# Layer 0 attention's last head and its row norm: squares and the weight row taken in column groups

## The reference, cut to what matters

```python
def rmsnorm(x, w, eps=1e-5):
    return (x * rsqrt(mean(x * x, axis=-1) + eps)) * w

x = layernorm(x)                                  # 625 x 768
qkv = rmsnorm(x, norm1_w) -> 12 heads of 64 columns
attn = softmax(qkv @ qkv.T / 8);  attn_out = attn @ qkv
out = x + attn_out                                # called z in the kernel
xf = rmsnorm(out, norm3_w)                        # called xf in the kernel
logits = xf @ gate_w.T ...                        # router, shared expert, 8 experts, top 2
```

## Time and profile before

| what | value |
|---|---|
| median of 3 runs | 1630.15 us (1621.01 to 1632.26) |
| the profiled execution | 1624.75 us |
| its span | 1623.2 us |
| TensorE busy | 1474.0 us, 91% |
| VectorE busy | 1275.0 us, 79% |
| ScalarE busy | 873.8 us, 54% |
| GpSimd busy | 331.8 us, 20% |
| granted TensorE clock, mean | 0.961 |

### The profile page before, as it was taken

The page is one execution under the profiler, slowest core; times in us unless marked ns, Lnnn a source line. Parts: engine busy times, 40 slices in busy tenths (PEclk is TensorE's granted clock), DMA queues, the critical chain, the costliest instruction groups (busy, mean ns, idle before and its releaser), DMA issues.

```text
span 1623.2 us, 36989 instructions
## 1 busy us (share of the span) xinstructions
PE 1474.0 (91%) x14673; PEld 1270.6 (78%) x14673; DVE 1275.0 (79%) x2196; ACT 873.8 (54%) x1235; POOL 331.8 (20%) x254
## 2 busy tenths in 40 slices
PE   7988868886999999999999889965999999999996
PEld 5666646664667899999999654445999999999995
DVE  8997767775565588888888779867988888888785
ACT  1113247775544567777665235554656666666651
POOL 0000405664030000000004037754600000000040
PEclk9999889998899999999999889978999999999999
DMA  7640000002375679888986011125888888888883
GB/s 201 159 120 1 1 10 1 1 1 79 120 223 174 229 277 289 305 308 292 296 301 225 26 32 33 33 88 195 294 304 290 297 286 301 297 293 291 296 264 102
DMA packets 55556, 297.61 MB, mean 183 GB/s; under 512 B 14063, under 2 KB 14319, under 8 KB 32433
## 3 DMA queue, kind: packets, MB, share of 16 engines
q1 hardware_dynamic: 41761, 263.23, 47.6%
q0 software_dynamic: 13712, 33.26, 7.5%
HBM read 264.07 MB, written 32.34 MB: 183 GB/s over the span
## 4 chain that ended last, share of the span: by engine, by line
PE 59%; DVE 7%; POOL 3%; ACT 2%; issue 2%; DMA 2%; SPq 0%; DVEq 0%; ACTq 0%
PE ps L744 14%; PE ps L723 9%; PE ps L725 9%; PE ps L727 9%; PE ps L2243 5%; PE ps L2226 5%; POOL wl L997 2%; PE ps L2355 2%; DMA ext<-in_units 2%; PE ps L756 1%; DVE wl L600 1%; PE ps L707 1%; DVE big L1875 1%; PE ps L2327 1%; PE ps L2297 1%
## 5 line engine op out<-in xcount | busy, mean ns | idle before, releaser
L723 PE MATMUL ps<-big,wh 128*128 128x176 f16 x2160 | 495.4, 239 | 10.6 <-DVE wl L600 8.5
L727 PE MATMUL ps<-big,wl 128*128 128x176 f16 x2160 | 495.4, 238 | 0.0
L725 PE MATMUL ps<-big,wh 128*128 128x176 f16 x2160 | 495.4, 238 | 0.0
L744 PE MATMUL ps<-big,wh 128*128 128x176 f16 x2160 | 262.8, 238 | 3.3 <-DVE big L634 3.3
L744 PE MATMUL ps<-big,wl 128*128 128x176 f16 x1080 | 248.9, 239 | 0.0
L600 DVE SCALAR_TENSOR_TENSOR wl<-ext,wh 128x2304 f16<-128x2304 f32 x90 | 229.6, 2552 | 1.7 <-issue 1.5
L600 DVE SCALAR_TENSOR_TENSOR wl<-raw,wh 128x2304 f16<-128x2304 f32 x90 | 229.5, 2550 | 0.0
L519 ACT ACTIVATE wh<-raw 128x2304 f16<-128x2304 f32 x90 | 190.6, 2119 | 59.2 <-PE ps L744 53.6
L723 PEld LDWEIGHTS ps<-big,wh 128*128 128x128 f16 x2160 | 208.3, 96 | 15.1 <-DVE wl L600 8.9
L519 ACT ACTIVATE wh<-ext 128x2304 f16<-128x2304 f32 x90 | 190.6, 2118 | 50.5 <-PE ps L744 33.1
L725 PEld LDWEIGHTS ps<-big,wh 128*128 128x128 f16 x2160 | 210.8, 98 | 0.2
(11 more groups left out here) (363 smaller groups left out, 2839.1 us busy)
## 6 DMA issues: line engine op xcount, KB each, us to landing
raw<-in_units SPq DMA_DIRECT2D x54, 1152.0 KB
ext<-in_units SPq DMA_DIRECT2D x54, 1152.0 KB
raw<-in_units SPq DMA_DIRECT2D x36, 1153.0 KB, 6.7
ext<-in_units SPq DMA_DIRECT2D x36, 1153.0 KB, 7.1
raw<-in_units_s SPq DMA_DIRECT2D x16, 769.0 KB, 4.5
ext<-in_units_s SPq DMA_DIRECT2D x16, 769.0 KB, 4.4
x_slots<-raw SPq DMA_DIRECT2D x1, 8976.0 KB
big<-x_slots POOLq DMA_DIRECT2D x17, 528.0 KB, 8.6
```

What stands on the lines that cost most here:

```text
L723: nc.tensor.matmul(o, wh[:, u % RING, w_], x_, start=c == 0 and m == 0, stop=False, skip_group_check=True)
L725: nc.tensor.matmul(o, wh[:, u % RING, w_], xTl[:, c, 0:ph.n], start=False, stop=False, skip_group_check=True)
L727: ins = nc.tensor.matmul(o, wl[:, u % RING, w_], x_, start=False, stop=c == KC - 1, skip_group_check=True)
L744: ins = nc.tensor.matmul(o, l_[:, u % RING, w_], r_, start=first and k == 0 and c % 2 == 0, stop=last and k == 2, skip_group_check=True)
```

## The change

Columns are cut at 256, 512, 704 and 768 (`PARTS`), that is behind heads 3, 7, 10 and 11.

- ScalarE squares columns 0 to 255 during head 6 and columns 256 to 511 during head 10, one tile in each step, behind that step's `weight_high`. It squares columns 512 to 703 behind the last `weight_high`, once head 10 has been added, and columns 704 to 767 behind the fence. The sums go to `st`, one number for each tile and group, and VectorE adds the four of them (a new reduction ahead of `mean_squares`).
- `sum_out(10)` is moved ahead of the last `weight_high` on ScalarE.
- VectorE computes `xf = z * vec` for columns 0 to 703 as soon as head 10 has been added. For head 11 the steps `fin` and `head_joined` are replaced by five VectorE instructions that multiply from PSUM and add into `z`. Then it computes the last 64 columns of `xf`. All of this stands ahead of the fence.
- `squares_asked` is gone. The scratch place of the fifth tile's squares moves to column 6700 of `big`.

```diff
+PARTS = (0, 4 * HD, 8 * HD, 11 * HD, D)
...
             weight_low(H * NT - 1)
             head_joined(H - 2)
-            head_joined(H - 1)
             fence(pool, F_MHA)
...
-            def squares():
-
-                count["sq"] += 1
-                act.wait_ge(s_var, count["sq"])
-                for t in range(NT):
-                    ins = nc.scalar.activation(junk[t], z[:, t, :], ACT.Square, accum_out=rs[:, 0, t:t + 1])
-                ins.then_inc(s_sq, 1)
+            def squares(g, t):
+
+                own = slice(PARTS[g], PARTS[g + 1])
+                nc.scalar.activation(junk[t][:, own], z[:, t, own], ACT.Square,
+                                     accum_out=st[:, t, g, 0:1]).then_inc(s_part, 1)
...
                 if t == 0 and h >= 2:
                     sum_out(h - 2)
+                if h in (6, 10):
+                    if t == 0:
+                        act.wait_ge(s_madd, h - 2)
+                    squares((h - 6) // 4, t)
+            sum_out(H - 2)
             weight_high(H * NT - 1)
-            sum_out(H - 2)
+            act.wait_ge(s_madd, H - 1)
+            for t in range(NT):
+                squares(2, t)
             sum_out(H - 1)
             fence(act, F_MHA)
...
-            squares()
+            act.wait_ge(s_madd, H)
+            for t in range(NT):
+                squares(3, t)
             root()
...
-                count["sq"] += 1
-                dve.wait_ge(s_sq, count["sq"])
+                dve.wait_ge(s_part, 4 * NT)
+                step(nc.vector.tensor_reduce(rs[:, 0, :], st[:, :, :, 0], AX.X, ALU.add))
                 nc.vector.tensor_scalar(rs[:, 0, :], rs[:, 0, :], 1.0 / D, eps, ALU.mult, ALU.add)\
...
             fin(H - 2)
-            fin(H - 1)
+
+            def row_weighted(n0, n1):
+
+                for t in range(NT):
+                    ins = nc.vector.tensor_tensor(xf[:, t, n0:n1], z[:, t, n0:n1], vec[:, 0, n0:n1], ALU.mult)
+                return ins
+
+            dve.wait_ge(s_vec[0], 32)
+            dve.wait_ge(s_madd, H - 1)
+            row_weighted(0, PARTS[3])
+            dve.wait_ge(s_mback, H)
+            for t in range(NT):
+                ins = nc.vector.scalar_tensor_tensor(
+                    out=z[:, t, PARTS[3]:D], in0=bank(7)[0:P, 128 + t * HD:128 + (t + 1) * HD],
+                    scalar=cols[:, 4 + (H - 1) % 2, t:t + 1], in1=z[:, t, PARTS[3]:D], op0=ALU.mult, op1=ALU.add)
+            ins.then_inc(s_madd, 1)
+            dve.wait_ge(s_madd, H)
+            step(row_weighted(PARTS[3], D))
             fence(dve, F_MHA)
...
-            squares_asked()
-            dve.wait_ge(s_vec[0], 32)
-            for t in range(NT):
-                ins = nc.vector.tensor_tensor(xf[:, t, :], z[:, t, :], vec[:, 0, :], ALU.mult)
-            step(ins)
             mean_squares(1e-5)
```

More of the change, by code:

```diff
@@ L159, in bass_gnn_moe_stack @@
         xsl = region(big, KC * T // 2, KC * T // 2).bitcast(F16).rearrange("p (c n) -> p c n", c=KC)
-        junk = [big[0:P, (t if t < 4 else 6) * D:((t if t < 4 else 6) + 1) * D] for t in range(NT)]
+        junk = [big[0:P, (t * D if t < 4 else 6700):(t * D if t < 4 else 6700) + D] for t in range(NT)]
         yT = region(big, 0, KC * B).rearrange("p (c n) -> p c n", c=KC)
@@ L327, in bass_gnn_moe_stack @@
         s_rowsok = sem("s_rowsok")
+        s_part = sem("s_part")
         s_tp = sem("s_tp")
@@ L1344, in mean_squares @@
                 root_of(rs[:, 3, :])
-            def squares_asked():
-                nc.vector.tensor_scalar(rs[:, 2, :], rs[:, 3, :], 1.0, None, ALU.mult).then_inc(s_var, 1)
             def rows_low(half):
```

## The result

The changed kernel took 1627.52 us (median of 20 runs, 1618.7 to 1631.99), the kernel before 1631.85 us beside it (20 runs, 1621.01 to 1636.47). The two medians differ by 4.3 us. That it lies so near 1627.52 is in part luck: the kernel before has medians of 1631.85 here and of 1628.09, 1628.02 and 1630.28 beside the experiments, so such a median moves by some us from one set of runs to the next.

A forecast was written before the change was run, and what follows sets the result against it. It took the single-file chain of waits from the last head to the first transpose as exposed; 0.9 - 0.3 + 2.9 - 0.3 = 3.2 us off the median 1630.15 gave 1627.0 us, range 1618 to 1632.

The forecast's parts named there:

- The copy: ScalarE's copy of head 10 ahead of the last rounding starts the last head's 20 matmuls 0.9 us earlier (0.8 to 0.95).
- The last head on VectorE: Between turning back and squares: multiply-adds and last products take 2.15 us against 1.83, a loss of 0.3 us.
- both ties: VectorE's 704-column products end at 392.48, a tie with the turning back at 392.43; no cost if both hold.
- The squares behind the fence: Five ScalarE squares of 64 columns take 1.3 us where 4.24 stood: 2.9 us saved.
- The squares in the heads: Ten squares of 256 columns inside heads 6 and 10 on ScalarE: 0.15 us lost per head, 0.3 in all.
- The rival that put all of them in line: All ten squares in the heads delay the chain: 4.2 us lost against 3.5 won, 1630.9 us; chance 0.12 (half or more).
- The weights: Their load behind the fence starts about half a microsecond earlier and stays hidden ahead of the first transposes, by less.
- The sum: All terms from the last heads to the first transpose: 0.9 - 0.3 + 2.9 - 0.3 = 3.2 us gained.
- Not swallowed at once: Rival: gain swallowed later, at a transfer or VectorE wait in the experts; time stays at 1630.2 us; chance 0.08.
- the rival of the clock: Shared expert's second up-matmul group: TensorE's clock drop vanishes (1.7 us won) or doubles (1.7 lost); chance 0.1 either side.

The follow-up runs named there:

- squares_only: Changed kernel with head 10's copy back behind the last rounding, last head's addition and weight row as before; ratio to the kernel before 0.9988 (0.9973 to 1.0003).

## Why the prediction was right, by its steps

- **The copy, 0.9 us: 0.8.** 5.92 to 5.12 us from the last exponential to the last head's matmuls. The next wait was GpSimd's remainders, as said; the hop from GpSimd to TensorE took 0.14 and not 0.07.
- **The last head on VectorE, 0.3 us lost: 0.15.** 1.98 us against 1.83. The multiply-adds took 1.05 (forecast 1.1), the products 0.77 (0.8), the products of 704 columns 4.10 (4.09), and both ties held. The formulas of the Trainium skill (VectorE: DVE Perf Modes, the section on the TRN2 errata) had given an estimate of 1.6 us for the two in place of my 1.9; the trace has 1.82, nearer to the rows' estimate.
- **The squares behind the fence, 2.9 us: 2.93.** 395.16 to 399.42 was 4.26, 392.56 to 393.89 is 1.33. `squares_only` showed that this term stands on the weight row's move: without it 0.9 are left.
- **The squares in the heads, 0.3 us lost:** 0.2 between the first two traces, within the spread of the others. The rival that put all of them in line (4.2 us) has fallen.
- **The weights:** they stayed hidden, as said. The gap from the squares' start behind the fence to the first transpose shrank from 8.0 us to 5.1, and the first products of the shared expert still follow the transposes without a gap (below).
- **The sum, 3.2 us:** 0.81 - 0.15 + 2.93 = 3.59 on the meter, less the 0.2 in the heads: 3.4.
- **Not swallowed at once.** From the first transpose to the first product of the shared expert it is 9.4 us before and 9.1 after.
- **The clock.** I had placed the rival of the clock at the shared expert and left it out of the sum. The group that took 4.56 us took 2.89 in the changed kernel, but the group ahead of it grew from 3.24 to 3.58:

```profile
406.95 3.58 PE ps L2242 x18
410.53 3.43 PE ps L2214 x60
413.96 2.89 PE ps L2242 x18
```

A single group of 18 matmuls therefore says little. From the first transpose to the end of the second group the kernel before took 20.8, 19.4, 20.9 and 19.4 us in its four traces and the changed one 19.2 in both of its own. So the good side of the rival (1.7 us) came true against two of the four traces, and hardly anything of it against the other two. What I had missed was the last head. The two traces of the kernel before that escape the fall there are the two that take 20.8 and 20.9 in the shared expert. Both stages together, from the last exponential to the end of the second group, took 41.5, 43.0, 41.6 and 42.9 us before and 36.3 twice after, so 5.2 to 6.7 less, where the terms of the sum account for 3.6. The rest I put down to the clock, since the instructions of the shared expert are the same. It rests on two traces of the changed kernel; in the other five with the early copy, transposes to second group took 19.2 to 20.6 us.

- **What stays open.** Behind that mark the span had another 1199.2 to 1207.0 us in the traces of the kernel before and 1209.7 and 1207.3 in those of the changed one. That spread is larger than the whole gain. So the 4.7 us (2.6 to 6.9) can't be divided among the stages: 3.4 lies in the interval, and so does 3.4 with a part of what the clock gave. My 3.2 had nothing for the clock in it, so that it lies inside the interval shows the terms to be of the right size and does not settle the clock's share.

## What to carry to other kernels

Where engines hand a result on in single file, price each step from the trace, and ask of each moved piece what lay beside it: grouping the squares was worth 2.9 us with the weight row moved ahead of the fence and 0.9 without. Look for idle time of an engine ahead of the chain into which a copy or a table load fits. And when an effect is 0.3% of the time, measure it between two marks in the trace, in more than one execution, as one pair of traces showed the changed kernel slower by 3 us where the medians have it faster by 4. A group of matmuls that speeds up is no gain as long as the one ahead of it may have slowed down: sum over the whole stage.

## What the runs showed of the hardware

The granted clock fell in the last head's matmuls in four of seven traces with gaps of 2.15 and 0.63 us around the turning back, and in none of seven with gaps of 0.47 and 1.50 us; a fall there cost 1.5 to 2.9 us. The same kernel, unaltered, took 17.9 to 23.0 us for one stretch of small matmuls: the granted clock was 0.5 (the 1.2 GHz level) for its first two to three us in the traces with 17.9 and 18.0, and for its first 15 us in those with 23.0 and 22.9. The Trainium skill (TensorE: Matmul & The Clock Gate, the part on the HAM clock gate) says that the monitor doesn't start with the kernel, so the same code can meet it differently in each run; the four traces of the kernel before agree, with a fall in the last head in two of them.
